# Projections and the turn of the maxima as two column halves in an attention and mixture-of-experts kernel

## The reference, cut to what matters

```
xq, xk, xv = (einsum('bsh,oh->bso', h, w).reshape(1, 16, 2048, 64) for w in (wq, wk, wv))
scores = softmax(einsum('bhid,bhjd->bhij', xq, xk) * 64**-0.5)
x = x + ga * (einsum('bhij,bhjd->bhid', scores, xv).reshape(1, 2048, 1024) @ wo.T)
h = layernorm(x) * (1 + cb) + sb
x = x + gb * (silu(h @ sw1.T) * (h @ sw3.T) @ sw2.T          # the shared expert
              + sum over the 2 chosen experts e of weight[e]*(silu(weight[e]*h @ w1[e].T) * (weight[e]*h @ w3[e].T)) @ w2[e].T)
```

## Time and profile before

| | |
|---|---|
| median of 3 runs | 1387.61 us (1387.3 to 1387.88) |
| the profiled execution | 1388.47 us, of which the span of its instructions is 1386.7 us |
| TensorE busy | 1361.5 us (98%), in 7850 passes |
| GpSimd busy | 1186.4 us (86%) |
| VectorE busy | 908.4 us (66%) |
| ScalarE busy | 663.7 us (48%) |
| chain that ended last | TensorE 93%, GpSimd 3%, VectorE 2%, ScalarE 1% |

### The profile page before, as it was taken

One profiled execution on the slowest core, in us unless ns is written; L12 is line 12 of the kernel. 1 busy time (PEld: TensorE's weight loads), 2 busy tenths in 40 slices (PEclk: granted clock), 3 DMA queues, 4 the chain that ended last, 5 costly groups with the idle time before them and its releaser, 6 DMA issues.

```text
span 1386.7 us, 19883 instructions
## 1 busy us (share of the span) xinstructions
PE 1361.5 (98%) x7850; PEld 697.3 (50%) x7850; DVE 908.4 (66%) x1023; ACT 663.7 (48%) x837; POOL 1186.4 (86%) x537
## 2 busy tenths in 40 slices
PE   7999999999999999999999999999999999999898
PEld 5444545454554545454454545454545545454565
DVE  6767666676767676676767676666767676746554
ACT  6444444444544445444544445445445444464331
POOL 2499999898989899999989898998989898989443
PEclk9999999999999999999999999999999999999999
DMA  7010201020100202020200102020201001003231
GB/s 199 8 40 1 46 2 46 2 47 0 33 15 2 46 1 47 1 47 1 46 1 20 28 1 47 1 47 1 46 1 37 11 2 45 1 1 69 60 96 53
DMA packets 31950, 41.39 MB, mean 30 GB/s; under 512 B 4298, under 2 KB 15186, under 8 KB 31858
## 3 DMA queue, kind: packets, MB, share of 16 engines
q1 hardware_dynamic: 31714, 40.13, 12.1%
q10 hardware_dynamic: 144, 0.00, 0.0%
HBM read 13.70 MB, written 1.11 MB: 11 GB/s over the span
## 4 chain that ended last, share of the span: by engine, by line
PE 93%; POOL 3%; DVE 2%; ACT 1%; issue 0%; DMA 0%; SPq 0%; POOLq 0%; DVEq 0%
PE ps L1190 33%; PE ps L1114 14%; PE ps L1166 10%; PE ps L1172 8%; PE ps L1169 8%; PE ps L1093 5%; POOL acc L851 2%; PE ps L1096 2%; PE ps L1214 2%; PE ps L425 2%; PE ps L439 2%; PE ps L440 2%; PE ps L1203 2%; DVE peak_parts L924 1%; PE ps L1178 1%
## 5 line engine op out<-in xcount | busy, mean ns | idle before, releaser
L851 POOL TENSOR_TENSOR acc<-acc,probs 128x1024 f32<-128x1024 f32 x448 | 1066.6, 2381 | 92.6 <-ACT probs L786 32.1
L924 DVE TENSOR_REDUCE peak_parts<-ps 128x2 f32<-128x1024 f32 x512 | 621.7, 1216 | 312.7 <-PE ps L1114 311.0
L786 ACT ACTIVATE probs<-ps 128x1024 f32<-128x1024 f32 x512 | 502.5, 1029 | 394.6 <-PE ps L1172 326.2
L1190 PE MATMUL ps<-probs,v_sb 128*64 128x512 f32 x2048 | 501.2, 605 | 0.0
L1190 PEld LDWEIGHTS ps<-probs,v_sb 128*64 128x64 f32 x2048 | 124.3, 136 | 222.4 <-issue 168.0
L1166 PE MATMUL ps<-q_hi,d_hi 64*128 64x512 f32 x512 | 213.0, 416 | 0.0
L1166 PE MATMUL ps<-q_hi,d_swap_hi 64*128 64x512 f32 x512 | 212.9, 416 | 0.0
L1172 PE MATMUL ps<-q_hi,d_lo 64*128 64x512 f32 x512 | 200.5, 392 | 0.0
L1169 PE MATMUL ps<-q_lo,d_swap_hi 64*128 64x512 f32 x512 | 200.4, 391 | 0.0
L1169 PE MATMUL ps<-q_lo,d_hi 64*128 64x512 f32 x512 | 200.3, 391 | 0.0
L1172 PE MATMUL ps<-q_hi,d_swap_lo 64*128 64x512 f32 x512 | 200.3, 391 | 0.0
(11 more groups left out here) (146 smaller groups left out, 1062.4 us busy)
## 6 DMA issues: line engine op xcount, KB each, us to landing
k_swap_hi<-k_hi SPq DMA_DIRECT2D x64, 128.0 KB, 2.3
d_swap_hi<-d_hi SPq DMA_DIRECT2D x64, 128.0 KB, 2.3
d_swap_lo<-d_lo SPq DMA_DIRECT2D x64, 128.0 KB, 2.3
token_weights<-weights_dram SPq DMA_DIRECT2D x32, 256.0 KB, 3.3
probs<-in_L_ffn_w_dram SPq DMA_DIRECT2D x2, 512.0 KB, 5.9
shifts<-shift_sb SPq DMA_DIRECT2D x64, 2.0 KB
out_dram<-probs SPq DMA_DIRECT2D x4, 256.0 KB, 3.1
x_in<-in_L_attn_x_dram SPq DMA_DIRECT2D x1, 960.0 KB, 8.8
```

The source lines that it names most:

```text
L786: act.activation(probs[:, kt % PROBS, :], ps[:, 2 * place:2 * place + 2, :].rearrange("p a b -> p (a b)"), ACT.Exp, scale=SCALE).then_inc( ...
L851: pool.tensor_tensor(total, total if kt > 1 else probs[:, 0, :], probs[:, kt % PROBS, :], ALU.add).then_inc(added, 1)
L924: dve.tensor_reduce(peak_parts[:, :, i // STRETCHES, i % STRETCHES], ps[:, bank:bank + 2, :], AX.X, ALU.max).then_inc(peak_free, 1)
L1190: mm = pe.matmul(ps[at:at + HEAD_DIM, PV_BANK, :], v_sb[:, p, chunk_of(kt) * HEAD_DIM:(chunk_of(kt) + 1) * HEAD_DIM], probs[:, kt % PROBS, ...
```

## The change

- The q, k, v and output projections are issued as two products with 64 columns of weights each, at column positions 0 and 64, as P V is. A q or k job has eight products instead of four, v two instead of one, the output projection sixteen instead of eight. The turn of the maxima is a float32 product with the identity instead of a transpose; for it `peak` is 64 wide, filled with zeros once.
- In `side_jobs` the long jobs come ahead of the pair of their place. The turn moves from place 25 to 26, the output projection from 27 to 23.
- "step k" and "low k" move to the place of their k job and the next one, and some inversions and scalings one or two places up.
- Of the 36 items the shared experts of groups 0 and 1 come first, those of groups 2 and 3 before the routed items of groups 1 and 2. VectorE weighs the first three routed items, the third after item 2. The jobs tied to items move by one item.

The core of the diff:

```diff
-    {3: ("q", 0), 15: ("k", 0), 19: ("k", 1), 25: ("shift", 0), 27: ("out", 0)},
-    {3: ("q", 1), 7: ("v", 0), 25: ("shift", 0), 27: ("v", 1)},
+    {3: ("q", 0), 6: ("sum", 0), 15: ("k", 0), 19: ("k", 1), 23: ("out", 0), 26: ("shift", 0)},
+    {3: ("q", 1), 7: ("v", 0), 10: ("sum", 0), 26: ("shift", 0), 27: ("v", 1)},
 )
-SUM_PLACES = (6, 10)
 
 LOW_PLACES = (
-    {4: ("low q", 0), 16: ("step k", 0), 18: ("low k", 0), 20: ("step k", 1), 22: ("low k", 1)},
+    {4: ("low q", 0), 15: ("step k", 0), 16: ("low k", 0), 19: ("step k", 1), 20: ("low k", 1)},
     {4: ("low q", 1)},
 )
 INVERSES = 4
 SCALE_PLACES = (
-    {6: ("inv", 0), 7: ("inv", 1), 9: ("inv", 2), 11: ("inv", 3), 13: ("scale", 0)},
-    {10: ("inv", 0), 12: ("inv", 1), 15: ("inv", 2), 19: ("inv", 3), 21: ("scale", 0)},
+    {6: ("inv", 0), 8: ("inv", 1), 9: ("inv", 2), 11: ("inv", 3), 12: ("scale", 0)},
+    {10: ("inv", 0), 12: ("inv", 1), 14: ("inv", 2), 17: ("inv", 3), 19: ("scale", 0)},
 )
 
 COUNTED = ("q", "k", "v", "sum", "shift")
...
-    if sums:
-        places[SUM_PLACES[half]].append(("sum", 0))
+    for place, (kind, i) in LONG_JOBS[half].items():
+        if sums if kind in ("sum", "out") else pairs if kind == "shift" else project:
+            places[place].append((kind, i))
     if pairs:
         for i in range(EARLY_PAIRS, PEAK_PAIRS):
             places[2 * (i - EARLY_PAIRS) + 1].append(("pair", i))
     if early:
         for i in range(EARLY_PAIRS):
             places[2 * (PEAK_PAIRS - EARLY_PAIRS + i) + 1].append(("pair", i))
-
-    for place, (kind, i) in LONG_JOBS[half].items():
-        if sums if kind == "out" else pairs if kind == "shift" else project:
-            places[place].append((kind, i))
...
+        SEQUENCE = [(0, EXPERTS), (1, EXPERTS)] + [(0, e) for e in range(EXPERTS)] \
+            + [(2, EXPERTS)] + [(1, e) for e in range(EXPERTS)] + [(3, EXPERTS)] \
+            + [(g, e) for g in (2, 3) for e in range(EXPERTS)]
+        ITEMS = GROUPS * ALL
+        ROUTED = [m for m in range(ITEMS) if SEQUENCE[m][1] < EXPERTS]
+        FIRST_OF = [min(m for m in range(ITEMS) if SEQUENCE[m][0] == g) for g in range(GROUPS)]
+        LAST_OF = [max(m for m in range(ITEMS) if SEQUENCE[m][0] == g) for g in range(GROUPS)]
+
+        FIRST_WEIGHED = ROUTED[:3]
 
...
+            earlier_items = [n for n in ROUTED if n < m and n % 2 == m % 2]
+            if earlier_items:
+                eng.wait_ge(ups, earlier_items[-1] + 1)
...
+                if m + 2 in FIRST_WEIGHED[2:]:
+                    weigh_tokens(dve, m + 2, weighted_first)
...
-                        at = i * BANK + k * P
-                        mm = pe.matmul(job.ps[:, k * P:(k + 1) * P], w[:, at:at + P], h_head[:, :],
-                                       start=True, stop=True)
+                        for at in (0, HEAD_DIM):
+                            col = i * BANK + k * P + at
+                            mm = pe.matmul(job.ps[at:at + HEAD_DIM, k * P:(k + 1) * P], w[:, col:col + HEAD_DIM],
+                                           h_head[:, :], start=True, stop=True, tile_position=(0, at))
                 if kind == "v":
-                    mm = pe.matmul(job.ps, h_head[:, :], wvT[:, i * BANK:(i + 1) * BANK], start=True, stop=True)
+                    for at in (0, HEAD_DIM):
+                        mm = pe.matmul(job.ps[at:at + HEAD_DIM, :], h_head[:, at:at + HEAD_DIM],
+                                       wvT[:, i * BANK:(i + 1) * BANK], start=True, stop=True, tile_position=(0, at))
                 mm.then_inc(job_full, 1)
 
             def pair(i, pairs_earlier, target_head, target_parity, target_half, bank, banks_used=1):
...
-                pe.transpose(job.ps[0:8, 0:P], peak[:, :], ident[:, :]).then_inc(job_full, 1)
+                pe.matmul(job.ps[0:HEAD_DIM, 0:P], peak[:, :], ident[:, :], start=True, stop=True,
+                          tile_position=(0, 0)).then_inc(job_full, 1)
...
-                        mm = pe.matmul(job.ps[:, 0:DIM], oT[:, half, k * P:(k + 1) * P], wo2[:, 4 * half + k, :],
-                                       start=(half == 0 and k == 0), stop=(half == 1 and k == 3))
+                        for at in (0, HEAD_DIM):
+                            col = k * P + at
+                            mm = pe.matmul(job.ps[at:at + HEAD_DIM, 0:DIM], oT[:, half, col:col + HEAD_DIM],
+                                           wo2[:, 4 * half + k, :], start=(half == 0 and k == 0),
+                                           stop=(half == 1 and k == 3), tile_position=(0, at))
```

More of the change, by code:

```diff
@@ L163, in build @@
         peak_parts = sb("peak_parts", [P, 2, PEAK_PAIRS // STRETCHES, STRETCHES])
-        peak = sb("peak", [P, 8])
+        peak = sb("peak", [P, HEAD_DIM])
         shift_sb = sb("shift_sb", [8, 2, P], F32R)
@@ L389, in banks @@
             return ps[:, 2 * (m % 2), :], ps[:, 2 * (m % 2) + 1, :]
-        ORDER = [EXPERTS] + list(range(EXPERTS))
-        def routed(m):
[L396 to L406, removed]
+        SEQUENCE = [(0, EXPERTS), (1, EXPERTS)] + [(0, e) for e in range(EXPERTS)] \
[6 more added lines that the diff above has]
+        FIRST_WEIGHED = ROUTED[:3]
+        def routed(m):
+            return ROUTED.index(m)
+        SUM_AFTER, INVERT_AFTER, SCALE_AFTER, PROJECT_AFTER, ADD_AFTER = 4, (4, 5), 6, 7, 7
+        STATS_AFTER, ROOT_AFTER, RSTD_AFTER, NORM_AFTER = 8, 9, 9, 10
+        GATE_AFTER = (14, 15, 16, 17)
+        LATE_AFTER = {11: ("turn", 3), 13: ("logits", 1), 18: ("weights", 3)}
         def weigh_tokens(eng, m, signal):
-            g, e = m // ALL, ORDER[m % ALL]
+            g, e = SEQUENCE[m]
             eng.wait_ge(weights_loaded[e], 16 * (g + 1))
-            if m >= 3:
-                eng.wait_ge(ups, m - 1)
+            earlier_items = [n for n in ROUTED if n < m and n % 2 == m % 2]
+            if earlier_items:
+                eng.wait_ge(ups, earlier_items[-1] + 1)
             eng.tensor_tensor(weighted[m % 2], hT[:, g * BANK:(g + 1) * BANK], token_weight[e],
@@ L417, in down @@
             def down(m):
-                g, e = m // ALL, ORDER[m % ALL]
+                g, e = SEQUENCE[m]
                 if m == 0:
                     pe.wait_ge(tail_free, TAIL_PAIRED)
-                if m % ALL == 0 and g >= 2:
+                if m == FIRST_OF[g] and g >= 2:
                     pe.wait_ge(out_ready, g - 1)
@@ L425, in down @@
                     mm = pe.matmul(ps[:, 6 + g % 2, k * P:(k + 1) * P], inner_w[m % 2][:, k * P:(k + 1) * P],
-                                   w2T[:, e, :], start=(m % ALL == 0 and k == 0),
-                                   stop=(m % ALL == ALL - 1 and k == 3), skip_group_check=True)
+                                   w2T[:, e, :], start=(m == FIRST_OF[g] and k == 0),
+                                   stop=(m == LAST_OF[g] and k == 3), skip_group_check=True)
                 mm.then_inc(downs, 1)
             for m in range(ITEMS):
-                g, e = m // ALL, ORDER[m % ALL]
+                g, e = SEQUENCE[m]
                 rhs = hT[:, g * BANK:(g + 1) * BANK] if e == EXPERTS else weighted[m % 2]
                 if m in FIRST_WEIGHED:
-                    pe.wait_ge(weighted_first, m)
+                    pe.wait_ge(weighted_first, FIRST_WEIGHED.index(m) + 1)
                 elif e < EXPERTS:
@@ L522, in add_up @@
             def add_up(g):
-                dve.wait_ge(downs, ALL * (g + 1))
+                dve.wait_ge(downs, LAST_OF[g] + 1)
                 if g >= 2:
@@ L529, in add_up @@
                                   x_mid[:, 4 * g:4 * g + 4, :], ALU.add).then_inc(out_ready, 1)
-            for m in FIRST_WEIGHED:
+            for m in FIRST_WEIGHED[:2]:
                 weigh_tokens(dve, m, weighted_first)
@@ L563, in ffn_dve @@
                     gate(dve, link, 1, [GATE_AFTER.index(m)])
-                if m % ALL == 1 and g > 0:
-                    add_up(g - 1)
+                if m - 1 in LAST_OF:
+                    add_up(LAST_OF.index(m - 1))
             add_up(GROUPS - 1)
@@ L573, in spread_weights @@
                 if g > 0:
[L575 removed]
+                    sp.wait_ge(inner_w_ready, SEQUENCE.index((g - 1, e)) + 1)
                 sp.dma_start(token_weight[e], weights_dram[e:e + 1, g * BANK:(g + 1) * BANK].broadcast_to(
@@ L812, in _ @@
         def _(pool):
+            pool.memset(peak[:, :], 0.0)
             pool.memset(ident[:, :], 0.0).then_inc(consts, 1)
@@ L860, in _ @@
             for m in range(ITEMS):
-                if m not in FIRST_WEIGHED and ORDER[m % ALL] < EXPERTS:
+                if m not in FIRST_WEIGHED and SEQUENCE[m][1] < EXPERTS:
                     weigh_tokens(pool, m, weighted_ready)
```

3 lines of the change are left out of this document (1 added, 2 removed).

## The result

Before: 1387.74 us median (1387.3 to 1388.03, 4 runs). After: 1363.13 us (1362.54 to 1363.38, 4 runs), ratio 0.9822, 95% interval 0.9805 to 0.9839. The forecast was 1359.7 us with a range of 1354 to 1372: the time lies in the range and 3.4 us above the point. Two executions further down ran at a clearly lower granted clock (1390.53 us of third_ahead, 2142.04 us of the kernel before beside short_last) and are left out of the ratios. The profiled execution took 1362.54 us for a span of 1360.7.

The account below looks back on a forecast made before the run. The prediction took TensorE to set the pace, with GpSimd close behind. From a profiled 1388.47 us it took 21.9 for the loop and 6.0 for the items, giving 1360.6, or 1359.7 as median; range 1354 to 1372.

Parts of the forecast that it names:

- The steps: TensorE's loop: a long-job step becomes a plain step plus streaming, saving 1.53 us a head before a 0.07 charge.
- The price of a pair of column-half passes: TensorE's 128-column passes in column halves: taken as 0.107 us a pair, between nothing and 0.214.
- The rival that decides at 0.146: TensorE handed column-half passes too slowly; slower from 0.146 us a pair. Chances: 0.08 for 0.107 to 0.146, 0.09 halves in turn.
- "low k" ahead of the maximum: VectorE behind k jobs: the next maximum ends near T + 5.0, bank wanted at T + 4.98; charged 0.07 us a head.
- VectorE is late behind the k jobs: Rival: "low k" costs each of two pairs 0.75 us, the loop gains nothing, 1382 us; chance 0.04.
- GpSimd's bound: Rival in the loop: GpSimd's additions, 75.2 us a head, cap the gain at 1.76 a head; 1355 us; chance 0.07.
- The count of heads: Loop total: 1.53 less 0.07 us a head, times 15 heads, gives 21.9 us.
- The items: Experts' first items: 7.5 us of gap and low clock won, 1.5 charged against it, gain 6.0 us.
- The gap and the low clock: At the first items: TensorE idle for GpSimd's late weighing, then clock at 0.57 for 6.60 us; 7.5 us in all.
- the charge of 1.5: In the items: 1.3 us waiting for VectorE's third weighing plus 0.2 for the output projection's tiling changes.
- The meeting at the third weighing: VectorE's third weighing beside GpSimd's additions: ends near 1285.3, TensorE there at 1284.0; charged 1.3 us.
- The output projection's tiling: Output projection among whole-array items now changes the tiling twice; charged 0.2 us.

Follow-up runs that it names:

- third_ahead: The changed kernel with VectorE weighing all three items ahead of the first item, the third into a buffer of its own; 1363.84 us, ratio 0.9827.
- short_last: The changed kernel with GpSimd's additions 9 to 15 of the very last unit cut to 256 of 1024 columns; 1361.9 us, ratio 0.9812.
- halves_only: The kernel before with projections and turn as column halves, every job at its old place; 1382.81 us, ratio 0.9964.
- order_only: The kernel before with the new places and VectorE order, whole-array products and old order of items; 1393.17 us, ratio 1.0038.
- loop_only: The changed kernel with the experts' items in their old order and weighed as before; 1366.14 us, ratio 0.9844.
- short_adds: The changed kernel with GpSimd adding only 768 of 1024 columns of each tile after the first; 1362.10 us, one run.
- short_maxima: The changed kernel with VectorE taking maxima over only the first 256 of each 512 keys; 1356.69 us, one run.
- items_only: The kernel before with only the new order of the items and VectorE's third weighing; 1384.79 us, ratio 0.9977.
- short_both: The changed kernel with GpSimd additions of 768 columns and VectorE maxima over half the keys; 1309.72 us, one run.

## Why the prediction came out as it did

**The steps: right.** Steps with a q, k or v job were to last 4.98 us and last 4.98 or 4.99, with the output projection 5.84 against 5.86, plain ones 4.12 against 4.12. What a head gains was to be 1.46 us and is 1.44 over 13 heads. halves_only and order_only show that it takes both parts: the forms alone give 0.07 a job (1388.05 - 1382.81 = 5.2 us in all), the places alone cost 1393.17 - 1388.05 = 5.1, and together they give 1388.05 - 1366.14 = 21.9 (loop_only). The reason is the one that the prediction gives: with the new form the job shares P V's tiling, and with the new place the pair shares that of the scores. With the form alone the pair still stands alone between two changes; with the place alone the job does, VectorE's hold takes what the pair saves, and the turn loses most of 5 us.

**The price of a pair of column-half passes: right.** I took 0.107 us. From the first of the 16 passes of a q job to the pair behind them 0.98 us pass (692.79 to 693.77), 0.12 over the 0.86 that eight pairs make at 0.107. The first of two changes is gone and the other is in there. The output projection with its 32 passes has 1.85 (753.74 to 755.59), so the eight further pairs take 0.87, 0.109 each, and no change of tiling is in that difference. The rival that decides at 0.146 would have made it 1.17 or more. The Trainium skill ("TensorE: Matmul & The Clock Gate", "Wait — 56ns, not 53.3ns?") gives some 62 ns for each matmul with hardware decode off; the output projection's 32 passes would then take 1.98 us, and the trace has 1.85 with the change of tiling in it. So that pace didn't bind here; whether hardware decode was on no run shows.

**"low k" ahead of the maximum: right for all heads but the first.** Steps with k jobs last as long as those with q jobs, and the pair behind one starts 1.81 us behind the other. Behind the second k job the prediction put the cost at nothing because the output projection, 1.72 long, stands there. The first head has none, and its pair waits 0.71 us: the wait that the rival "VectorE is late behind the k jobs" put at 0.75, once instead of thirty times. order_only, loop_only and short_adds, which have the new places, show the same wait there (0.72, 0.71, 0.70), halves_only and the kernel before don't.

**GpSimd's bound: right in that it isn't reached, and in how near it is.** Its wait was to fall to about 0.4 and is 0.34; short_adds shows no gain in the loop from a faster GpSimd, short_maxima a GpSimd that bounds as soon as VectorE doesn't. (The bound by the rows is 76.98 - 75.2 = 1.78 us a head; the prediction has 1.76.)

**The count of heads: 2 us too much.** "(1.53 - 0.07) x 15 heads = 21.9". The 13 whole heads gave 18.66 us where that term has 19.0. What lies ahead of and behind them gave 19.93 - 18.66 = 1.3 where the term has 2.9. Of the missing 1.6 us, 0.8 are the step of 4.90 us in the first head, 0.2 were lost before the first P V (54.90 against 54.70), and 0.2 are the last head's output projection, which is still to come at the place compared. 21.73 us stand in the two traces at the first item and look like a hit; 1.7 of them are the dip of the clock before.

**The items: mis-sized, 6.0 against 4.3.** The gap and the low clock went, as forecast (7.5 us), and the idle time that is left before item 4 was to be 1.3 us and is 1.59. The failed term is the charge of 1.5 against that gain; it should have been 3.2 (7.5 - 4.3), and the traces show three parts of it. Two are meetings of a VectorE product of two inputs in SBUF with work of GpSimd.

- The meeting at the third weighing cost 2.4 where 1.3 was charged. The prediction let the weighing end late, but took the product ahead of it (L551) at the 0.69 us of the earlier trace rows; it took 1.47, made TensorE wait another 0.30, and pushed the weighing behind it. The two waits are 1.9 us; by the starts around them (1260.42 to 1261.74 to 1264.50 to 1265.46 after, 1260.50 to 1261.36 to 1262.25 to 1263.11 in short_last) TensorE loses 0.46 + 1.87 + 0.10 = 2.4, so the other 0.5 is starting anew behind them. short_last, without the meeting, is 2.4 us shorter in the items, so the whole gain would have been 6.7.
- The meeting at the shared item of group 2 cost 0.8 and was in no term. Of the other groups' order the prediction looked only at the time between a weight's transfer and its use.
- The output projection's tiling was charged 0.2 and cost 0.1: from the product ahead of it to the first product of the next item 4.43 us pass after (1274.49 to 1278.92) and 4.31 before (1298.82 to 1303.13).

That makes 3.3 against the 3.2. In the kernel before, VectorE's products at 1279.16 and 1281.95 cost nothing by luck of timing: each started as one of GpSimd's additions ended and ahead of the next (1279.28, 1282.21), and it was these additions that took 2.79 and 2.63 us instead of 2.36. After, the one at 1260.22 started in the middle of an addition (1258.78 to 1261.14) and ended 0.55 us behind it. In third_ahead, where the weighing is out of the way, another product pays.

**The sum.** 1388.47 - 19.9 - 1.7 (the dip) - 4.3 = 1362.6, and 1362.54 was measured; the forecast had 21.9 and 6.0. The medians differ by 24.6 us, where the forecast had 27.9. The change's own two terms came out 3.7 us short, both in the same direction; between the two profiled executions (25.9 us) 1.7 of that is covered by luck, the dip of the clock that only the one before has.

What stays open: the 0.2 us ahead of the first P V, another 0.4 at the two ends of the loop, and why the clock dips in some executions and not in others.

## What to carry to other kernels

Work in a tiling of its own costs its streaming plus a change on either side, and so does whatever stands alone between two such pieces; changing its form pays only when its place changes too, so try the two together before giving up on either (here -5.2 and +5.1 us apart, -21.9 together). When a stretch is short, ask which two engines read SBUF in it, and which of them starts first: moving a product off one place makes the next one pay, unless the other engine's work ends earlier. When an overlap is said to cost nothing because another job stands beside it, look for the round of the loop that lacks this job (here the first head, 0.71 us). And before a difference of 1 to 2 us between two traces is put down to a change, look at the granted clock by windows in both.

## What the runs showed of the hardware

- A VectorE product of two inputs in SBUF (128x512, 0.69 us by itself) took 1.47, 2.71 and 2.83 us beside GpSimd's additions of 128x1024 (2.35 to 2.39 us each), and 0.69 again when these were out of the way (short_last) or when it started ahead of one (before, 1279.16 and 1281.95; there the addition took 2.79 and 2.63). Beside GpSimd's weighing of 128x512 (1.26) it took 1.80. A product with one input in PSUM took 0.69 in the middle of an addition (1259.50). The Trainium skill ("SBUF — State Buffer", "SBUF: two separate sides") says that whichever of the two starts first holds the pair of ports for its whole instruction and the other blocks. The traces agree: of the two it is the one that started second that was longer. 2.83 is 0.69 and nine tenths of an addition.
- The granted clock dipped by 1.7 us' worth late in the loop in some executions (0.83 over 1220 to 1230 us in loop_only, short_adds and third_ahead, over 1240 to 1250 in items_only and over 1250 to 1260 in order_only, 0.92 and 0.91 over 1230 to 1250 in halves_only, the two windows shown of before) with TensorE busy for all of the time, and not in others (the changed kernel's trace, short_last's, short_both's). Ahead of it TensorE had been busy for 8.48 of 10 us (1210 to 1220, before); the changed kernel's trace has 8.36 of 10 in the same place of the program, 1190 to 1200, and no dip behind it.
- An idle time of 1.59 us among the items left the clock at 1.00; one of 2.71 with 1.29 ahead of it left 0.72 over 6 us; 4.65 had left 0.57.
- 16 passes of 128 columns in column halves, each with its own weights, run in fp32 at 0.107 to 0.109 us a pair (0.98 us for 16 with a change of tiling, 1.85 for 32), which is the pace of whole-array passes of 128 columns.
